# Perceiver layer on one core: the shared gated unit taken out of the per-tile periods and run tile by tile between the last tile and the experts

## The chip, the cores and the metric

The kernel runs on one core of one Trainium2 chip. The metric is the device time of the program in microseconds (us); the lower, the better. Three runs of the kernel before gave 1420.79, 1424.43 and 1424.91 us, median 1424.43 us. A further execution was profiled: every row below is from it.

## The reference, cut to what matters

The input `x` is 64 sequences of 32 rows of 256 numbers, 2048 rows in all. Each goes through cross attention to a context, a small self attention with ternary weights, and a feed-forward layer with 8 experts and one shared gated unit. Only the last matters for the change:

```python
def _moe(x, Wg, W1, W3, W2, sw1, sw3, sw2):
    ...
    probs = jax.nn.softmax(xt @ Wg, axis=-1)
    eidx = jnp.argmax(probs, axis=-1)
    ...
    pos = (jnp.cumsum(oh, axis=0) * oh).sum(-1) - 1
    keep = pos < C
    ...
    xd = jnp.zeros((E * C, d), x.dtype).at[flat].set(xt, mode='drop')
    h = jax.nn.silu(jnp.einsum('ecd,edh->ech', xd, W1)) * jnp.einsum('ecd,edh->ech', xd, W3)
    oe = jnp.einsum('ech,ehd->ecd', h, W2).reshape(E * C, d)
    ...
    shared = jax.nn.silu(xt @ sw1) * (xt @ sw3) @ sw2
    return (out + shared).reshape(b, sl, d)
```

`xt` is the normalised row. The shared unit is the line `shared = ...`, with 352 hidden columns, padded to 384. The layer's residual is added to it.

## The kernel before, in words

The 2048 rows are 16 tiles of 128 rows. Work is cut into **periods**. A prologue prepares weights and the first half of tile 0. Then 15 equal periods follow (a hardware loop on each engine), in which the first half of the next tile (keys K0 to K7, queries Q and QP, scores s0 to s3, attended values o0 to o2) is interleaved with the second half of this tile: its last entry (pt3, o3), f (output projection and residual x1), xt1, qkv, qk, sc, pv (self attention), pr (projection and residual `x2`), ln2, xt2 (the normalised rows `xn2` turned into `xn2T`), lg (router), up and dn (the shared unit), pos (the place of each row in its expert's list) and scat (an indirect DMA that puts `xn2` into the experts' rows in DRAM). The last period has the second half of tile 15 alone. Then 8 experts run one after the other: turn the rows, two products up, the gate, one product down, gather what stands in `out`, add, and put back.

Everything is hand written: each engine is in order, and its order of steps within a period is a list (`ORDER`); the steps wait on semaphores. `filled[s]` counts fills of a PSUM bank by TensorE (PE), `drained[s]` its drains. Banks are "0" to "3" (tensor AB), "4" and "5" (C), "D" (Db) and "E" (Eb).

The names that the prediction uses, by engine, with lines of the profile:

- PE: rk2, s2, o0, xt2, rk3, lg, **up** (two products into banks 4 and 5: 24 records of 128x128, `C<-xn2T,sw`), s3 (`AB<-ctxT,qpT`), pt1 (transposes `C<-consts_sb,prob` L735, and a product into Db), **dn** (`Eb<-sw,hT`, 6 records of 128x256), pos, o1 (`Eb<-pT,cn_hi`), pt2, o2, and at the next period's start K0 (`AB<-wk_hi,c_hi`).
- ACT: rk3, oh0, **up** (a sigmoid made of Exp, Ln and Exp, L1025 to L1029), e2 (four Exp of scores), ph1 (high halves of probabilities), lg, tl1 (L938, `pTl<-Db`, which drains bank D of pt1), e3, oh1, ph2.
- DVE: do0, lg (ends with `onehot`, L1650), **up** (two products, L1655 and L1658), s3 (starts with the memset of `junk` at L1307, then four products, then `nbias`), i2 (L1533, `sinv`), **dn** (L1680), dp1 (low halves, drains banks 4 and 5 of pt1), pos (ends with `slot_s`, L1675), do1, dp2, i3.
- POOL: c3, n2 (waits for i2; starts at L1124, ends with `plast` L1179; pt2 waits for it), scat (L1210), h0 of the next period (ends with `c_lo`, L1130; K0 waits for it), n3.
- SP issues the loads and, at the end of the loop's body, `store_base`: the finished rows `base` go to `out`.

In the prologue an all-zero tile, which `base` lends, clears the experts' rows in DRAM.

## Time and profile before

| what | value |
|---|---|
| median of three runs | 1424.43 us (1420.79 to 1424.91) |
| the profiled execution's own time | 1421.66 us |
| its span in the trace | 1419.8 us |
| mean granted TensorE clock | 0.962 |
| busy: PE, DVE, ACT, POOL | 89%, 65%, 62%, 40% of the span |
| matmul instructions | 10526 |
| DMA | 55.18 MB, 39 GB/s over the span |

### The profile page before, as it was taken

How to read it: one execution, taken by the hardware profiler on the slowest of the kernel's cores; microseconds unless marked ns; L12 is line 12 of the kernel's file. 1: busy time of each engine (PE TensorE's matmuls, PEld its weight loads, DVE VectorE, ACT ScalarE, POOL GpSimd, SP SyncE). 2: the span in 40 equal slices, each digit the busy share in tenths (PEclk: the TensorE clock that was granted, in tenths of full speed). 3: DMA queues.
4: the chain of work that ended last, by engine and by line, in shares of the span. 5: the costliest groups of instructions: out<-in, count | busy, mean ns of one | idle time of the engine just before them, and what ended most of it. 6: DMA issues, size and time to landing. Idle time of an engine off the chain costs nothing.

```text
span 1419.8 us, 34906 instructions
## 1 busy us (share of the span) xinstructions
PE 1270.2 (89%) x10526; PEld 853.6 (60%) x10526; DVE 916.5 (65%) x3313; ACT 884.8 (62%) x3728; POOL 574.4 (40%) x1371
## 2 busy tenths in 40 slices
PE   4877999999999999999999999999999999984596
PEld 1644666666665656666666666665656666653485
DVE  6754776767676767676776767676767676763132
ACT  4455676758576766767676758576666767661132
POOL 3044262534435352526262534435352526244143
PEclk9888999999999999999999999999999999996699
DMA  9100010101010000001010101000000001210351
GB/s 370 57 17 15 13 36 11 34 11 34 8 27 18 23 23 16 22 11 34 11 34 11 34 11 34 8 27 19 23 22 16 22 11 34 93 51 1 74 189 47
DMA packets 36130, 55.18 MB, mean 39 GB/s; under 512 B 6748, under 2 KB 29433, under 8 KB 35040
## 3 DMA queue, kind: packets, MB, share of 16 engines
q1 hardware_dynamic: 31632, 46.53, 10.5%
q0 software_dynamic: 3376, 7.98, 1.6%
q14 instruction: 52, 0.43, 0.1%
q8 instruction: 14, 0.23, 0.1%
q10 hardware_dynamic: 1056, 0.02, 0.0%
HBM read 46.54 MB, written 8.42 MB: 39 GB/s over the span
## 4 chain that ended last, share of the span: by engine, by line
PE 52%; DVE 17%; issue 9%; ACT 8%; POOL 4%; DMA 1%; POOLq 0%; DVEq 0%; ACTq 0%
PE AB L595 27%; PE Db L595 9%; PE Eb L595 7%; DVE kst L1351 3%; PE C L595 3%; DVE rq L1408 2%; PE C L720 2%; PE C L735 2%; POOL prob L1169 2%; ACT AB L946 2%; ACT prob L1014 2%; DVE pT L1538 2%; DVE px L1620 1%; ACT wt_q L938 1%; ACT rkb L1008 1%
## 5 line engine op out<-in xcount | busy, mean ns | idle before, releaser
L946 ACT ACTIVATE AB<-AB 128x128 f32<-128x128 f32 (+1 forms) x1160 | 303.3, 261 | 105.0 <-PE AB L595 101.7
L1124 POOL TENSOR_TENSOR pjunk<-pjunk 128x1 f32<-128x1 f32 x289 | 57.5, 199 | 681.4 <-DVE sinv L1533 386.4
L1351 DVE BATCH_NORM_STATS2 kst<-AB 128x6 f32<-128x256 f32 x512 | 181.7, 416 | 107.1 <-PE AB L595 102.0
L595 PE MATMUL AB<-wk_hi,c_hi 128*128 128x512 f16 x512 | 199.4, 389 | 19.1 <-POOL c_lo L1130 7.3
L946 ACT ACTIVATION_READ_ACCUMULATOR AB<-AB 128x1 f32 (+1 forms) x1160 | 215.6, 186 | 0.0
L595 PE MATMUL AB<-wk_lo,c_hi 128*128 128x512 f16 x512 | 197.8, 386 | 0.0
L595 PE MATMUL AB<-wk_hi,c_lo 128*128 128x512 f16 x512 | 197.7, 386 | 0.0
L1014 ACT ACTIVATE prob<-prob,nbias,rq 128x257 f32<-128x257 f32 x256 | 150.6, 591 | 8.4 <-DVE nbias L1528 8.4
L1169 POOL TENSOR_SCALAR prob<-prob,sinv 128x257 f32<-128x257 f32 x256 | 129.7, 507 | 20.2
L595 PE MATMUL AB<-ctxT,qpT 128*128 128x257 f32 x512 | 123.2, 383 | 11.5 <-ACT pxT L1046 11.5
L595 PEld LDWEIGHTS AB<-wk_hi,c_hi 128*128 128x128 f16 x512 | 50.9, 99 | 101.2 <-issue 29.3
L595 PEld LDWEIGHTS AB<-ctxT,qpT 128*128 128x128 f32 x512 | 92.3, 190 | 26.0 <-ACT pxT L1046 15.5
L1008 ACT COPY rkb<-C 128x512 f32<-128x512 f32 x128 | 69.3, 596 | 55.7 <-PE C L720 54.8
L595 PE MATMUL Eb<-pT,cn_hi 128*128 128x512 f16 x256 | 88.8, 386 | 8.8 <-DVE o_halves L1543 5.3
L1522 DVE CUSTOM_DVE_ANT_0 prob<-AB,rkb 128x257 f32<-128x257 f32 x256 | 94.1, 422 | 0.0
L1538 DVE TENSOR_TENSOR pT<-C,pT 128x512 f16<-128x512 f32 x128 | 82.2, 683 | 11.7 <-ACT pT L985 10.4
L595 PEld LDWEIGHTS AB<-wk_hi,c_lo 128*128 128x128 f16 x512 | 51.0, 100 | 63.1 <-issue 4.7
L595 PE MATMUL Db<-wvo_hi,o_halves 128*128 128x256 f16 x512 | 86.5, 273 | 0.7 <-ACT o_halves L978 0.7
L595 PE MATMUL AB<-x_hi,wqk_hi 128*128 128x128 f16 x512 | 86.9, 219 | 0.0
L595 PE MATMUL AB<-x_lo,wqk_hi 128*128 128x128 f16 x512 | 86.8, 219 | 0.0
L595 PE MATMUL AB<-x_hi,wqk_lo 128*128 128x128 f16 x512 | 86.8, 219 | 0.0
L735 PE MATMUL C<-consts_sb,prob 128*128 128x128 f32 x512 | 69.0, 278 | 17.8 <-POOL plast L1179 17.8
(282 smaller groups left out, 2873.9 us busy)
## 6 DMA issues: line engine op xcount, KB each, us to landing
ctxT<-in_ctxT SPq DMA_DIRECT2D x64, 128.5 KB, 2.1
ctxn<-in_ctxn SPq DMA_DIRECT2D x64, 128.0 KB, 2.1
expert_rows<-base POOLq DMA_DIRECT2D x1, 2048.0 KB, 15.6
xin<-in_x SPq DMA_DIRECT2D x16, 128.0 KB, 2.2
prob<-in_wqT SPq DMA_DIRECT2D x1, 2048.0 KB, 20.3
xres<-in_x SPq DMA_DIRECT2D x16, 128.0 KB, 2.1
out<-base SPq DMA_DIRECT2D x16, 128.0 KB, 1.7
wq_hi<-in_w SPq DMA_DIRECT2D x2, 768.0 KB, 4.5
```

Source lines behind the costliest of these rows:

```text
L595: return pe.matmul(out, lhsT, rhs, start=start, stop=stop)
L720: ins = pe.transpose(C[:, n, KT * P * (g % 2) + P * tt:KT * P * (g % 2) + P * (tt + 1)], rkx[:, b % 2, tt, P * g:P * (g + 1)], ident)
L735: ins = pe.transpose(C[:, tt, P * g:P * (g + 1)], prob[:, b, g, P * tt:P * (tt + 1)], ident)
L946: ins = nc.scalar.activation(k, k, ACT.Square, accum_out=sums[0:m, h:h + 1])
L1008: nc.scalar.copy(rkb[:, b % 2, 2 * n:2 * n + 2, 0:KT * P], C[:, n].rearrange("p (g n) -> p g n", g=2)).then_inc(drained[s].sem, 1)
L1014: ins = nc.scalar.activation(prob[:, b, g], prob[:, b, g], ACT.Exp, bias=nbias[:, b, g:g + 1], scale=rq[:, G * b + g:G * b + g + 1], accum ...
L1124: own.mark(pool.tensor_tensor(pjunk[:, 0:1], pjunk[:, 1:2], pjunk[:, 1:2], ALU.mult))
L1169: ins = pool.tensor_scalar(prob[:, b, g], prob[:, b, g], sinv[:, b, g:g + 1], P_SCALE, ALU.mult, ALU.mult)
L1351: ins = V.bn_stats(stats[:, 0, 2 * half + n], AB[0:m, 2 + half, 2 * D * n:2 * D * (n + 1)])
L1408: ins = V.tensor_scalar(rq[SQ * m:SQ * (m + 1), G * b:G * (b + 1)], src, 1.0 / WQK_SCALE, None, ALU.mult)
L1522: V.tensor_tensor_reduce(prob[:, b, g], AB[:, g, 0:SKV], rkb[:, b % 2, g], 1.0, BELOW, ALU.mult, ALU.max, smax[:, b, g:g + 1]).then_inc(dr ...
L1538: V.tensor_tensor(pT[:, b % 2, 1, tt], C[:, tt], pT[:, b % 2, 0, tt], ALU.subtract).then_inc(drained[s].sem, 1)
```

## The change

The shared unit leaves the periods. In a period only its inputs are kept: when tile n's `x2` and `xn2T` are ready, SP stores `x2` to `out` and `xn2T` to spare DRAM (`store_halfway`), where `base` was stored before. The two products up (`shared_up`, U0 to U15), the sigmoid (`shared_sigmoid`), the gate (`shared_hidden`), the product down (`shared_down`, D0 to D15) and the sum (`shared_sum`) of all 16 tiles run in the last period, in an order of its own, `LAST_ORDER`: U0 to U7 and D0 to D5 stand between the steps of tile 15, and U8 to U15 and D6 to D15 behind its last step, ahead of the experts. The operands come back from DRAM into the unused ends of four weight tensors (`turned`, `back`), four tiles ahead; the sum is written in place and stored to `out`. U uses banks 0 to 3 in pairs (U4: banks 4 and 5). The experts' rows are loaded behind D9's store. POOL's gathers wait for all 16 stores.

```diff
     "PE": """K0 pt3 K1 X K2 o3 K3 f Q xt1 K4 qkv QP rk0 s0 qk sc rk1 K5 K6 K7 pt0 pv s1 st pr rk2 s2 o0 xt2 rk3
-              lg up s3 pt1 dn pos o1 pt2 o2""".split(),
+              lg s3 pt1 pos o1 pt2 o2""".split(),
     "ACT": """K0 tl3 K1 X ph3 K2 oh3 K3 gKN0 Q xt1 gRQ K4 qkv gqkv QP rk0 qk e0 rk1 K5 sc K6 K7 ph0 gKN1 pv tl0
-              rk2 e1 xt2 rk3 oh0 up e2 ph1 lg tl1 e3 oh1 ph2 tl2 oh2""".split(),
+              rk2 e1 xt2 rk3 oh0 e2 ph1 lg tl1 e3 oh1 ph2 tl2 oh2""".split(),
     "DVE": """K0 X K1 XL dp3 K2 K3 KN0 do3 kn0 f Q RQ K4 rq qkv qr s0 sc K5 i0 sm K6 K7 KN1 dp0 kn1 ys yv s1 pr
-              ln2 i1 s2 do0 lg up s3 i2 dn dp1 pos do1 dp2 i3 do2""".split(),
+              ln2 i1 s2 do0 lg s3 i2 dp1 pos do1 dp2 i3 do2""".split(),
     "POOL": """h0 n3 h1 X h2 c0 c1 r0 cl ln1 r1 h3 n0 r2 y r3 ln2 c2 n1 c3 n2 scat""".split(),
+}
+
+
+BANK_PAIRS = ["01", "23", "01", "23", "45"] + ["01", "23"] * 6
+LAST_ORDER = {
+    "PE": """U0 pt3 U1 o3 f D0 U2 xt1 D1 qkv U3 D2 qk sc U4 D3 pv U5 st pr D4 U6 xt2 lg D5 U7 pos D6 U8 D7 U9 D8 U10 D9
+             U11 D10 U12 D11 U13 D12 U14 D13 U15 D14 D15""".split(),
+    "ACT": """tl3 ph3 U0 oh3 U1 xt1 U2 qkv gqkv U3 qk sc U4 pv U5 xt2 U6 lg U7 U8 U9 U10 U11 U12 U13 U14 U15""".split(),
+    "DVE": """dp3 U0 do3 f U1 D0 qkv U2 D1 qr U3 D2 sc sm U4 D3 ys yv pr ln2 U5 D4 lg U6 D5 pos U7 D6 U8 D7 U9 D8
+              U10 D9 U11 D10 U12 D11 U13 D12 U14 D13 U15 D14 D15""".split(),
+    "POOL": """n3 ln1 y ln2 scat""".split(),
...
+            def store_halfway(p):
+                sp.wait_ge(drained["E"].sem, drained["E"].at(p, "pr"))
+                sp.dma_start(d["out"][bass.ds(p.tile * P, P), :], x2[:]).then_inc(x2_out.sem, 16)
+                sp.wait_ge(drained["D"].sem, drained["D"].at(p, "xt2"))
+                sp.dma_start(turned_rows[bass.ds(p.tile * P, P), :], xn2T[:].rearrange("p k n -> p (k n)")).then_inc(xn2T_out.sem, 16)
...
+            def load_rows():
+                sp.wait_ge(scattered.sem, scattered.at(LAST, "scat"))
+                for e in range(E):
+                    sp.dma_start(xrows[e], xd_rows[e * CAP:(e + 1) * CAP, :].rearrange("(p a) c -> p a c", p=P))\
+                        .then_inc(rows_in[e], 16)
+
+            def load_turned(n):
+                sp.dma_start(turned[n % 4].rearrange("p k n -> p (k n)"), turned_rows[n * P:(n + 1) * P, :])\
+                    .then_inc(turned_in[n % 4], 16)
+
+            def load_back(n):
+                sp.dma_start(back[n % 4], d["out"][n * P:(n + 1) * P, :]).then_inc(back_in[n % 4], 16)
+
             sp.wait_ge(filled["3"].sem, filled["3"].at(p, "QP"))
+            for n in range(4):
+                sp.wait_ge(xn2T_out.sem, 16 * (n + 2))
+                load_turned(n)
+                sp.wait_ge(x2_out.sem, 16 * (n + 2))
+                load_back(n)
             for e in range(4):
                 load_up(e)
             sp.wait_ge(filled["3"].sem, filled["3"].at(p, "K7"))
@@ -570,11 +618,21 @@
             sp.wait_ge(filled["5"].sem, filled["5"].at(p, "rk3"))
             for e in range(2, 4):
                 load_down(e)
-            store_base(p)
-            store_base(LAST)
-            sp.wait_ge(scattered.sem, scattered.at(LAST, "scat"))
-            for e in range(E):
-                sp.dma_start(xrows[e], xd_rows[e * CAP:(e + 1) * CAP, :].rearrange("(p a) c -> p a c", p=P)).then_inc(rows_in[e], 16)
+            store_halfway(p)
+            sp.wait_ge(xn2T_out.sem, xn2T_out.at(p, "o"))
+            sp.wait_ge(x2_out.sem, x2_out.at(p, "o"))
+            for n in range(TILES):
+                s = BANK_PAIRS[n][1]
+                sp.wait_ge(filled[s].sem, filled[s].at(LAST, f"U{n}"))
+                if n + 4 < TILES - 1:
+                    load_turned(n + 4)
+                sp.wait_ge(drained["E"].sem, drained["E"].at(LAST, f"D{n}"))
+                sp.dma_start(d["out"][n * P:(n + 1) * P, :], back_of(n)).then_inc(sum_out[n % 4] if n < TILES - 1 else last_out, 16)
+                if n + 4 < TILES - 1:
+                    sp.wait_ge(sum_out[n % 4], 16 * (n // 4 + 1))
+                    load_back(n + 4)
+                if n == 9:
+                    load_rows()
...
+            def shared_up(p, n):
+                if n < TILES - 1:
+                    pe.wait_ge(turned_in[n % 4], 16 * (n // 4 + 1))
+                else:
+                    pe.wait_ge(drained["D"].sem, drained["D"].at(p, "xt2"))
+                for w, s in enumerate(BANK_PAIRS[n]):
+                    pe.wait_ge(drained[s].sem, drained[s].turn(p, f"U{n}"))
+                    up(lambda f: bank[s][:, P * f:P * (f + 1)], sw13, w, turned_of(n)).then_inc(filled[s].sem, 1)
...
+            def shared_down(p, n):
+                s = BANK_PAIRS[n][1]
+                pe.wait_ge(drained[s].sem, drained[s].at(p, f"U{n}"))
+                start(p, f"D{n}")
                 for f in range(FC):
-                    ins = mm(Eb[:, 0:DIM], hT[:, f], sw2[:, f], start=f == 0, stop=f == FC - 1)
+                    ins = mm(Eb[:, 0:DIM], uhT[n % 2][:, f], sw2[:, f], start=f == 0, stop=f == FC - 1)
...
+            def shared_sigmoid(p, n):
+                s = BANK_PAIRS[n][0]
+                act.wait_ge(filled[s].sem, filled[s].at(p, f"U{n}"))
+                if n >= 2:
+                    s2 = BANK_PAIRS[n - 2][0]
+                    act.wait_ge(drained[s2].sem, drained[s2].at(p, f"U{n - 2}"))
+                sigmoid(p, n, flat2(usig[n % 2]), bank[s][:, 0:FC * P]).then_inc(sig_ready.sem, 1)
...
+            def step_xt2(p):
+                act.wait_ge(xn2T_out.sem, xn2T_out.before(p))
+                drain(p, "xt2", "D", flat2(xn2T), Db[:, 0:DIM])
...
-            pool.wait_ge(base_out.sem, base_out.at(LAST, "o"))
+            for k in range(4):
+                pool.wait_ge(sum_out[k], 16 * len(range(k, TILES - 1, 4)))
+            pool.wait_ge(last_out, 16)
...
+                dve.wait_ge(x2_out.sem, x2_out.before(p))
...
+            def shared_hidden(p, n):
+                first, second = BANK_PAIRS[n]
+                hidden, n_cols = all_of(uhT[n % 2]), FC * P
+                dve.wait_ge(sig_ready.sem, sig_ready.at(p, f"U{n}"))
+                if n >= 2:
+                    dve.wait_ge(filled["E"].sem, filled["E"].at(p, f"D{n - 2}"))
+                V.tensor_tensor(hidden, bank[first][:, 0:n_cols], all_of(usig[n % 2]), ALU.mult).then_inc(drained[first].sem, 1)
+                dve.wait_ge(drained[first].sem, drained[first].at(p, f"U{n}"))
+                dve.wait_ge(filled[second].sem, filled[second].at(p, f"U{n}"))
+                V.tensor_tensor(hidden, hidden, bank[second][:, 0:n_cols], ALU.mult).then_inc(drained[second].sem, 1)
+
+            def shared_sum(p, n):
+                dve.wait_ge(filled["E"].sem, filled["E"].at(p, f"D{n}"))
+                if n < TILES - 1:
+                    dve.wait_ge(back_in[n % 4], 16 * (n // 4 + 1))
+                V.tensor_tensor(back_of(n), back_of(n), Eb[:, 0:DIM], ALU.add).then_inc(drained["E"].sem, 1)
```

Three places, as the order of the built programs shows them.

TensorE (PE) near the end of the loop's body, before: lg (`Db<-wg`), up, s3, pt1, dn, pos.

```order
L595 MATMUL Db<-wg,xn2T 128x8 x2
L854 REGISTER_ALU
L595 MATMUL C<-xn2T,sw 128x128 x12
L726 REGISTER_ALU
L595 MATMUL AB<-ctxT,qpT 128x257 x4
L733 REGISTER_ALU
L735 MATMUL C<-consts_sb,prob 128x128 x8
L595 MATMUL Db<-ident,plast 12x128 x4
L592 REGISTER_ALU
L595 MATMUL Eb<-sw,hT 128x256 x3
L595 MATMUL Db<-onehot,consts_sb 128x8
```

The same place in the changed program:

```order
L653 MATMUL Db<-wg,xn2T 128x8 x2
L784 REGISTER_ALU
L653 MATMUL AB<-ctxT,qpT 128x257 x4
L791 REGISTER_ALU
L793 MATMUL C<-consts_sb,prob 128x128 x8
L795 REGISTER_ALU
L653 MATMUL Db<-ident,plast 12x128 x4
L650 REGISTER_ALU
L653 MATMUL Db<-onehot,consts_sb 128x8
```

Both products of the shared unit are gone; s3 stands right behind lg, and pos right behind pt1.

VectorE (DVE) at the same place, before: the end of lg (`onehot`), up, and the start of s3.

```order
L1649 CAST eidx<-idx 128x1
L136 REGISTER_ALU
L1650 TENSOR_SCALAR onehot<-consts_sb,eidx 128x8
L1655 TENSOR_TENSOR hT<-C,sig 128x384
L1656 REGISTER_ALU
L1657 REGISTER_ALU
L1658 TENSOR_TENSOR hT<-hT,C 128x384
L1516 REGISTER_ALU
L1519 REGISTER_ALU
L1307 MEMSET junk 128x1
```

The same place in the changed program:

```order
L1725 CAST eidx<-idx 128x1
L136 REGISTER_ALU
L1726 TENSOR_SCALAR onehot<-consts_sb,eidx 128x8
L1590 REGISTER_ALU
L1591 REGISTER_ALU
L1594 REGISTER_ALU
L1382 MEMSET junk 128x1
```

s3 follows `onehot` directly. All else that stands around it on DVE is as it was.

TensorE in the last period, before, from xt1 on (`wt_q` is sc, `pxT,vals` is pv, `wproj` is pr):

```order
L604 MATMUL Eb<-consts_sb,xn 128x128 x2
L595 MATMUL Db<-wqkv,xn1T 128x384 x2
L788 MATMUL C<-consts_sb,heads 128x128 x8
L595 MATMUL AB<-wt_q 32x32 x64
L595 MATMUL AB<-pxT,vals 32x128 x16
L595 MATMUL Db<-ones,px 128x1
L595 MATMUL Eb<-wproj,pxT 128x256 x4
```

And in the changed program, from D0 on (a product of x12 into AB or C is a U, one of x3 into Eb is a D):

```order
L653 MATMUL Eb<-sw,hT 128x256 x3
L653 MATMUL AB<-wqk_hi,sw 128x128 x12
L662 MATMUL Eb<-consts_sb,xn 128x128 x2
L653 MATMUL Eb<-sw,prob 128x256 x3
L653 MATMUL Db<-wqkv,xn1T 128x384 x2
L653 MATMUL AB<-wqk_lo,sw 128x128 x12
L653 MATMUL Eb<-sw,hT 128x256 x3
L846 MATMUL C<-consts_sb,heads 128x128 x8
L653 MATMUL AB<-wt_q 32x32 x64
L653 MATMUL C<-wq_hi,sw 128x128 x12
L653 MATMUL Eb<-sw,prob 128x256 x3
L653 MATMUL AB<-pxT,vals 32x128 x16
```

A product of another tile now stands between any two steps of tile 15 but qk and sc.

## Rows read from the trace of the kernel before

**Rows 1.** The page, busy us (share of span) and instructions by engine.

```profile
PE 1270.2 (89%) x10526; PEld 853.6 (60%) x10526; DVE 916.5 (65%) x3313; ACT 884.8 (62%) x3728; POOL 574.4 (40%) x1371
```

**Rows 2.** Waits of TensorE, 268 to 1268 us: us in total, times, longest.

```profile
PE AB L595 <- POOL c_lo L1130: 6.7, 13, 0.6
```

**Rows 3.** Timeline of PE, one period's end: start, us, what [idle before].

```profile
1174.09 1.04 PE L720 MATMUL C<-consts_sb,rkx 128*128 128x128 f32 x8
...
1179.71 2.94 PE L595 MATMUL C<-xn2T,sw 128*128 128x128 f32 x24
1182.49 1.90 PE L595 MATMUL AB<-ctxT,qpT 128*128 128x257 f32 x8
...
1185.52 1.56 PE L595 MATMUL Eb<-sw,hT 128*128 128x256 f32 x6
...
1187.78 0.38 PE L595 MATMUL Eb<-pT,cn_hi 128*128 128x512 f16 x1
...
1189.63 1.09 PE L735 MATMUL C<-consts_sb,prob 128*128 128x128 f32 x8 [0.18 <-POOL plast L1179]
...
1193.28 0.39 PE L595 MATMUL AB<-wk_hi,c_hi 128*128 128x512 f16 x1 [0.39 <-POOL c_lo L1130]
```

**Rows 4.** Timeline of PE, rk2 of the following period.

```profile
1249.80 1.04 PE L720 MATMUL C<-consts_sb,rkx 128*128 128x128 f32 x8
```

**Rows 5.** Timeline of DVE at the same place.

```profile
1182.41 0.47 DVE L1650 TENSOR_SCALAR onehot<-consts_sb,eidx 128x8 f32<-128x8 f32 x1
...
1184.40 0.06 DVE L1307 MEMSET junk<- 128x1 f32 x1 [0.18 <-DVE hT L1658]
...
1186.14 0.17 DVE L1533 RECIPROCAL sinv<-ssum 128x4 f32<-128x4 f32 x1
```

**Rows 6.** Timeline of ACT at the same place: the sigmoid's last step, and tl1.

```profile
1182.43 0.52 ACT L1029 ACTIVATE sig<-sig 128x384 f32<-128x384 f32 x1
...
1186.35 0.56 ACT L938 CAST pTl<-Db 12x512 f16<-12x512 f32 x1
```

**Rows 7.** Timeline of POOL at the same place: n2's start, scat, h0's end.

```profile
1186.38 0.19 POOL L1124 TENSOR_TENSOR pjunk<-pjunk 128x1 f32<-128x1 f32 x1 [3.54 <-DVE sinv L1533]
...
1190.70 1.11 POOL L1210 DMA_INDIRECT expert_rows<-xn,slot_s  x1 [0.55 <-issue]
...
1192.47 0.68 POOL L1130 TENSOR_TENSOR c_lo<-ctxT,c_hi 128x257 f16<-128x257 f32 x1
```

**Rows 8.** Windows of PE: stretch and its us, PE busy, granted clock, DMA.

```profile
1268.00:1338.00 70.00, 31.80 (x294) 0.66 0.09 13
1157.00:1161.00 4.00, 4.00 (x15) 0.57 0.00 0
```

**Rows 9.** Timeline of PE, the last tile and the first expert.

```profile
1285.49 0.44 PE L604 MATMUL Eb<-consts_sb,xn 128*128 128x128 f32 x2 [2.48 <-DVE xn L1340]
...
1294.46 1.97 PE L788 MATMUL C<-consts_sb,heads 128*128 128x128 f32 x8 [5.81 <-DVE heads L1593]
1297.15 1.48 PE L595 MATMUL AB<-wt_q 16*32 16x32 f32 x105 [0.72 <-ACT wt_q L938]
...
1301.01 1.08 PE L595 MATMUL AB<-wt_q 16*32 16x32 f32 x18 [0.43 <-issue]
1307.78 1.05 PE L595 MATMUL AB<-pxT,vals 32*32 32x128 f32 x32 [5.68 <-DVE pxT L1615]
...
1318.26 0.69 PE L604 MATMUL Db<-consts_sb,xn 128*128 128x128 f32 x2 [2.53 <-DVE xn L1340]
...
1337.97 1.11 PE L899 MATMUL Eb<-consts_sb,rkb 128*128 128x128 f32 x4 [9.93 <-DMA rkb<-expert_rows]
1339.80 8.05 PE L595 MATMUL AB<-prob,wq_hi 128*128 128x256 f32 x24 [0.72 <-issue]
...
1349.01 5.42 PE L595 MATMUL AB<-prob,wq_lo 128*128 128x256 f32 x24 [0.72 <-ACT prob L938]
```

**Rows 10.** The page, DMA issues: KB each, median us to landing.

```profile
xin<-in_x SPq DMA_DIRECT2D x16, 128.0 KB, 2.2
```

More of the change, by code:

```diff
@@ L318, in build @@
         hT = sb("hT", [P, FC, P])
-        base = sb("base", [P, DIM])
         stats = sb("stats", [P, 6])
@@ L375, in build @@
         xres_in = Events(sem("xres_in"), 16, **fills)
-        base_out = Events(sem("base_out"), 16, pro=["none"], full=["o"], last=["o"])
+        x2_out = Events(sem("x2_out"), 16, pro=["none"], full=["o"])
+        xn2T_out = Events(sem("xn2T_out"), 16, pro=["none"], full=["o"])
+        back_in = [sem(f"back_in{k}") for k in range(4)]
+        turned_in = [sem(f"turned_in{k}") for k in range(4)]
+        sum_out = [sem(f"sum_out{k}") for k in range(4)]
+        last_out = sem("last_out")
         ctxT_in = [Events(sem(f"ctxT_in{b}"), 16, **fills) for b in range(NB)]
@@ L460, in build, with turned_of, back_of @@
         rest = [x[:, 2 * n:2 * n + 2, :].rearrange("p a n -> p (a n)") for x in (pxT, px) for n in range(8)]
+        bank = {s: AB[:, n] for n, s in enumerate(BANKS)} | {"4": C[:, 0], "5": C[:, 1]}
+        def turned_of(n):
+            return turned[n % 4] if n < TILES - 1 else xn2T
+        def back_of(n):
+            return back[n % 4] if n < TILES - 1 else x2[:]
         def wo_of(h):
@@ L1073, in _ @@
                 "pv": step_pv,
-                "xt2": lambda p: drain(p, "xt2", "D", flat2(xn2T), Db[:, 0:DIM]),
-                "lg": step_lg, "up": step_up,
-            }
+                "xt2": step_xt2,
+                "lg": step_lg,
+            }
+            for n in range(TILES):
+                steps[f"U{n}"] = lambda p, n=n: shared_sigmoid(p, n)
             steps |= {f"K{j}": (lambda p, j=j: square_keys(p, f"K{j}", P, kn2[:, H * j:H * (j + 1)])) for j in range(8)}
```

70 lines of the change are left out of this document (27 added, 43 removed).

## The prediction, made before the run

> **What bounds the kernel now.** I read the page first: TensorE is busy 89% of the span, the others 40 to 65% [rows 1]. That is a mean over three stages, so next I read one period on a timeline. From one rk2 to the next it is 1249.80 - 1174.09 = 75.7 us [rows 3, 4]. PE waits in it only in short pieces. The one that matters here is the wait of K0 for `c_lo` from POOL: 6.7 us in 13 periods, 0.5 each [rows 2]. It is short, but it says that POOL's chain ends later than PE's own at the seam of two periods: PE and a chain over DVE and POOL are nearly even there. So what leaves PE counts only as far as that chain gets shorter too. The third view is the last tile: 31.8 us busy of 70, at a mean clock of 0.66 [rows 8]; a chain of short steps with waits of 2.5 to 5.8 us between them, and 9.9 us for the experts' rows [rows 9]. There PE has room.
>
> **The periods.** At full clock up takes 1182.49 - 1179.71 = 2.78 us of PE, and dn 1.56 [rows 3]: 4.34 us per tile. Were PE alone the bound, 15 periods would give back 65.1 us. I follow the chain instead, in the times of [rows 3, 5 to 7].
> - PE: lg ends at 1179.7, s3 follows to 1181.5, pt1 to 1183.0.
> - DVE: `onehot` ends at 1182.9, as before, since do0 and lg depend on nothing that moved. s3 started at 1184.40; now at 1183.1, with the usual 0.2 us of issue. So s3 and i2 come 1.3 us earlier: `sinv` at 1184.8 for 1186.14.
> - POOL: n2 waits for i2 and starts at 1185.1 for 1186.38. It took until 1189.6, so now 1188.3. Scat waited a further 0.4 us for the slots; pos now has its input early, so scat moves by 1.7, and h0 ends at 1191.4 for 1193.15.
> - ACT: without the sigmoid (three steps of 0.5) e2 starts 2 us earlier. But tl1, which empties bank D for pos, still stands behind e2, ph1 and lg: `pTl` at about 1184.3 for 1186.35. So pos waits until 1184.9, and o1 follows to 1187.0. Its low half needs dp1, ready at 1186.2, hence no later.
> - PE again: pt2 waits for n2 until 1188.35 (before 1189.63), o2 ends at 1191.3, K0 starts with h0 at 1191.45 (before 1193.28).
>
> The seam moves by 1.8 us, not 4.3; the other 2.5 us reappear on PE as two gaps, of about 1.9 us ahead of pos and 1.3 us ahead of pt2. What comes behind K0 keeps its order and lengths. I take 1.75 per period, and 1.4 for the last one, which has no K0: 14 x 1.75 + 1.4 = **25.9 us off**. The bounds of this term: 1.3 per period (the DVE step alone), 19.5; and 4.34, 65.1. I stand near the lower one, as the row of POOL's wait [rows 2] is the nearest thing measured.
>
> The Trainium skill (Perfetto Trace Analysis, Identifying the Most-Contended Engine) says to optimise the engine with the highest occupancy first; for TensorE it distrusts that share as a distance to the limit. By the first half of this rule all 65.1 us would come off; the trace agrees on which engine is busiest, 89%, but its wait on `c_lo` speaks against the whole gain. It is a rival below.
>
> The new stores cost nothing that I can find. A 128 KB transfer lands in about 2.2 us [rows 10]; SP now issues two per period in place of one. Both sources are ready before SP comes to them (it waits for s3 first), so ctxn's last load behind them goes out earlier than behind `base`. DVE's pr and ACT's xt2 wait for the stores of the period before, landed 60 us earlier. If that cover went, a store would delay pr by its 2.2 us.
>
> **The last stretch.** I keep the old clock times, with the end of o2 at 1268.4, and lay LAST_ORDER over them. U0 fills the wait for n3; U1 ends at 1275.3; o3 and f run as before, f to 1283.0.
> - D0 and U2 stand ahead of xt1: 1283.0 + 1.56 + 2.78 = 1287.3, for 1285.49 (1.8 late). D1 stands ahead of qkv.
> - DVE does U2's gate (the 1.5 us between `onehot` and s3 in [rows 5]) and D1's sum ahead of qr: qk at 1297.1 for 1294.46 (2.6 late). sc starts at 1299.2 for 1297.15.
> - sc took 1302.09 - 1297.15 = 4.9 us, of which 1.8 are issue gaps and the rest ran at half clock; at full clock 3.3. It ends at 1302.5.
> - U4 and D3 (4.3 us) fit under the softmax; pv at 1308.2 for 1307.78.
> - U5, st, pr (half its time at full clock), D4, U6: xt2 at 1318.6 for 1318.26.
> - lg, D5, U7, pos: pos ends at 1324.7.
> - Ten D and eight U are left: 10 x 1.56 + 8 x 2.78 = 37.8 us, PE alone. ACT (three steps of 0.52, [rows 6]) and DVE (the gate's 1.5 us, and a sum that is smaller than either product) need less than the 4.3 us of a tile, and D of a tile stands behind U of the next, so their chains hide. D15 ends at 1362.7, with 0.2 of wait for its gate.
> - The experts' rows, asked for behind D9 (near 1340), land under U11 to U14, so the 9.9 us of waiting disappear. Bank E's drain, the turn and its copy take 2.0 us, and the first product up is at full clock, 5.2 us for 8.05. The turn and copy for the next take 1.3: the second expert's product starts at 1371.3, for 1349.01 before. From there all is as it was.
>
> That is **22.3 us on**. Not in it yet: around qk and sc PE does little for some 7 us, and there the clock will fall, as it did before; I add **2.5 us** (U4 and D3 partly at half clock, 4.3 us of work). Bounds of the whole term: no idle at all on PE (16 x 4.34 of shared unit, about 15.5 for tile 15 at full clock, 7.9 up to the second expert) gives 92.8 us for the stretch of 80.6, or 12.2 on; tile 15 at half clock throughout gives about 18 more than my 22.3, or 40.
>
> Loads: `turned` n + 4 is issued behind the store of tile n - 1, more than three tiles of 4.3 us ahead of its U, against 2.2 to land. The narrowest is tile 14: its load stands behind the eight loads of rows, issued near 1347, wanted near 1352.
>
> **Sum.** 1419.8 - 25.9 + 22.3 + 2.5 = 1418.7 us of span, and 1.9 around it: 1420.6. The profiled execution took 1421.66, and the median of the runs, 1424.43, is 2.8 above it; on that scale the sum would be 1423.4. I say **1421.5**: no change. A measurement of this kernel tells about 0.3% (4.3 us) from nothing.
>
> **The rivals.**
> - *The whole of PE's time comes off the periods.* For it: 89% busy, waits of a few tenths. Against it: pt2 and K0 already wait on POOL [rows 3]. It gives 1420.6 - 39.2 = 1381. Chance 0.06.
> - *The last stretch packs better* (no fall of the clock, gaps filled): down to the bound above, 1410.5; from 3.3 us of gain on it shows as faster. For it: PE has work at hand nearly everywhere. Chance 0.27.
> - *Slower: the new gaps make the clock fall in each period.* For it: the clock already fell in some periods without any long wait; at 1157 it was 0.57 over 4 us, with PE busy throughout [rows 8], right behind sc. Such a fall costs 1.7 us where PE is the bound. The two new gaps lie within 5 us of each other, and pt2, o2 behind them are on the path. At 1.5 us each, four more periods with a fall make it slower, all fifteen cost 22: up to 1443. Against it: they are shorter than the waits of 2.5 us and more behind which it fell in the last tile [rows 9], with two us of matmuls between them. Chance 0.15.
> - *Slower: the last stretch stays at 1.2 GHz* to about pos, as before, U and D then at double length: 1439. Against it: PE is now busy in most of the stretch. Chance 0.10.
> - The forecast, within 0.3%: 0.42.
>
> **How the numbers follow.** Faster 0.33 (the first two), same 0.42, slower 0.25. The range leaves out the first rival and most of the extreme ends of the two slower ones: 1404 to 1438. For the forecast alone, 1416 to 1427.
>
> **What the profile would show.** Right: a period of about 74 us; new waits of PE, for ACT's `pTl` ahead of pos and for `plast` ahead of pt2; K0 still waiting for `c_lo`; no wait for the experts' rows; 103 to 105 us from the last period's start to the second expert's product. Wrong: a period near 71.4 us (the chain had slack that I missed); granted clock below 1 around pt2 in most periods; waits of U or D on `turned` or `back`, which I put at none; issue gaps within U and D.

## The result, and the profile after

The changed kernel takes 1434.86 us (1430.49 to 1437.59, 6 runs), the kernel before in the same session 1422.61 (1420.35 to 1424.91, 6 runs): 1.0074 times, 95% interval 1.0057 to 1.0091, so 0.6 to 0.9% slower. The forecast was no change, 1421.5. The profiled execution took 1436.62 us, its span 1434.8 for 1419.8.

The page after, for [rows 1] (busy us, share of the span, instructions):

```profile
PE 1274.6 (89%) x10526; PEld 853.6 (59%) x10526; DVE 916.0 (64%) x3313; ACT 885.8 (62%) x3728; POOL 574.3 (40%) x1371
```

Shares tell nothing here: the two pages look alike. I cut both spans at DVE's step lg (its `onehot`), which every tile has, and at the second expert's first product.

| us of the profiled execution | before | after | forecast of the difference |
|---|---|---|---|
| to the first lg | 193.1 | 192.4 | 0 |
| 14 periods, lg to lg | 1065.0 | 1052.0 | -24.5 |
| last full tile's lg to the second expert's product | 90.8 | 119.6 | +23.4 |
| from there to the end | 70.8 | 70.7 | 0 |

(14 x 1.75 = 24.5; the forecast's -1.4 for the seam without K0 and its +24.8 for the last stretch make up the +23.4.) So the miss has two parts: the periods gave 11.5 us less than forecast, the last stretch cost 5.4 more. That these add up to 16.9 while the span is 16.1 above the forecast's 1418.7 is, but for rounding, the prologue's 0.7.

**The periods.** TensorE's waits after, 268 to 1250 us, for [rows 2] (us in total, times, longest):

```profile
PE Db L653 <- ACT pTl L1001: 21.6, 14, 1.9
PE C L793 <- POOL plast L1252: 20.8, 26, 1.5
PE AB L653 <- ACT wt_q L1001: 14.7, 13, 1.2
PE AB L653 <- ACT pxT L1113: 9.9, 13, 0.8
```

The two forecast gaps stand at the head of the list: for `pTl` ahead of pos (21.6 us in 14 waits, 1.5 each; forecast 1.9) and for `plast` ahead of pt2 (forecast 1.3). One thing differs from the forecast: PE no longer waits for `c_lo` ahead of K0. POOL's chain and PE's own now end together there, and the wait that bounds the period's end is the one for `plast`. The timeline of PE at one period's end, for [rows 3]:

```profile
1170.77 0.39 PE L653 MATMUL Db<-onehot,consts_sb 128*128 128x8 f32 x2 [1.45 <-ACT pTl L1001]
...
1174.58 1.09 PE L793 MATMUL C<-consts_sb,prob 128*128 128x128 f32 x8 [1.49 <-POOL plast L1252]
```

Periods in which the clock held are 74.0 us (median of 3) for 75.7 before (median of 10): 1.67 less, for 1.75 forecast. But only 3 of 14 held. In 11 the granted clock fell from 2.4 to 1.2 GHz, in the kernel before in 4, and within these periods it fell at one place, right behind sc. PE around such a fall, first the timeline, then windows (us from and to; us; busy time and instructions of PE, PEld, DVE, ACT, POOL; granted clock; DMA share; GB/s):

```profile
1066.37 1.28 PE L653 MATMUL AB<-wt_q 16*32 16x32 f32 x128 [1.12 <-ACT wt_q L1001]
1067.58 1.91 PE L778 MATMUL C<-consts_sb,rkx 128*128 128x128 f32 x8
1069.28 0.63 PE L653 MATMUL AB<-wk_hi,c_hi 128*128 128x512 f16 x1
```

```profile
1065.00:1067.50 2.50, 1.38 (x131) 1.17 (x129) 0.60 (x5) 2.50 (x7) 0.00 (x0) 1.00 0.15 45
1067.50:1071.00 3.50, 3.50 (x30) 2.29 (x18) 2.27 (x6) 2.17 (x8) 0.00 (x0) 0.53 0.00 0
1071.00:1074.00 3.00, 3.00 (x15) 1.42 (x14) 1.67 (x6) 3.00 (x20) 0.09 (x1) 0.98 0.00 0
```

PE waits 1.12 us for `wt_q`, then does 128 tiny products of 16x32 in 1.28 us, and then its clock is at 1.2 GHz for some 3.4 us with PE busy throughout. Both kernels have this place; nothing there was changed. 14 periods at 74.0 would be 1036; they took 1052, so the falls cost 16 us. In the kernel before 14 x 75.7 = 1060 stand against 1065: 5 us.

**The last stretch.** It begins with a fall that the count of 14 periods leaves out: behind the two new gaps of the last full tile the clock is at 1.2 GHz for 6.8 us, and from lg to the end of o2 it takes 11.2 us, where 10.3 less the forecast 1.4 had been laid out. That is 2.3 of the 5.4 us.

```profile
1250.07 1.97 PE L793 MATMUL C<-consts_sb,prob 128*128 128x128 f32 x8 [0.71 <-POOL plast L1252]
```

```profile
1248.60:1255.40 6.80, 6.09 (x22) 3.10 (x20) 2.49 (x7) 2.88 (x7) 4.01 (x11) 0.50 0.05 16
```

From there PE's walk went as laid out as far as qk, and then stopped:

```profile
1284.28 1.09 PE L846 MATMUL C<-consts_sb,heads 128*128 128x128 f32 x8 [1.63 <-issue]
1295.01 1.53 PE L653 MATMUL AB<-wt_q 16*32 16x32 f32 x128 [9.64 <-ACT wt_q L1001]
```

PE waits for ACT, but qk had been done since 1285.4. ACT, DVE and POOL at the same time:

```profile
1281.24 0.52 ACT L1092 ACTIVATE prob<-prob 128x384 f32<-128x384 f32 x1
1293.84 1.07 ACT L1001 COPY wt_q<-C 128x512 f32<-128x512 f32 x2 [12.08 <-remote]
```

```profile
1293.78 0.55 DVE L1737 TENSOR_TENSOR prob<-prob,AB 128x384 f32<-128x384 f32 x1 [9.08 <-remote]
```

```profile
1272.27 1.11 POOL L1287 DMA_INDIRECT expert_out<-tag,slots  x1 [0.16 <-issue]
...
1290.36 0.97 POOL L1287 DMA_INDIRECT expert_out<-tag,slots  x1 [0.30 <-issue]
```

ACT and DVE resume within 0.1 us of each other. "remote" means that the profile names no engine of the program as the releaser. All the while, until 1291.3, POOL writes the tags of tiles 0 to 14 (a tag tells the experts which token stands in a row, and its gate), one small indirect DMA every 1.28 us. SP's store of tile 1's sum was followed by the load that waits for it only 8.2 us later; in f1_no_tags below, without the fifteen writes, the same two stand 1.7 us apart.

```profile
1281.00 0.34 SPq L630 DMA_DIRECT2D out<-wq_lo  x1
1289.21 0.33 SPq L605 DMA_DIRECT2D wq_lo<-out  x1
```

The kernel before writes the same tags at the same point of its last tile; what they cost there is taken up below, with the experiments on the tags.

The rest of the stretch was close. Counted from the end of o2, pos ended 7.2 us later than laid out (63.5 us for 56.3). From pos to the end of D15 it took 36.5 us for 38.0: the unit took 2.68 + 1.30 us per tile on PE instead of 4.34, which over the last eight U and ten D is 34.4 us for 37.8, and some 2 us of waits stood between them. The experts' rows were waited for no more, and tile 14's `turned` came late by 0.8 us, the load named as the narrowest. 7.2 less 1.5, less the 2.5 us that the forecast had added for the clock, are the other 3.1 of the 5.4 us.

```profile
1345.13 2.94 PE L653 MATMUL AB<-wqk_hi,sw 128*128 128x128 f32 x24 [0.82 <-DMA wqk_hi<-expert_out]
...
1364.07 5.42 PE L653 MATMUL AB<-prob,wq_lo 128*128 128x256 f32 x24 [0.72 <-ACT prob L1001]
```

### The profile page after: what moved, and what is told of

Read it like the earlier page. It is cut to its first block, busy times and chain, and to the rows that moved or that the text cites. A ratio compares the mean times of both kernels' runs of the same rounds, so it can differ in the third digit from the quotient of the medians.

```text
span 1434.8 us, 35151 instructions
## 1 busy us (share of the span) xinstructions
PE 1274.6 (89%) x10526; PEld 853.6 (59%) x10526; DVE 916.0 (64%) x3313; ACT 885.8 (62%) x3728; POOL 574.3 (40%) x1371
## 4 chain that ended last, share of the span: by engine, by line
PE 42%; DVE 15%; POOL 13%; issue 13%; ACT 6%; DMA 1%; another core or an unknown queue 1%; POOLq 1%; SPq 0%; DVEq 0%; ACTq 0%
PE AB L653 26%; PE Db L653 8%; POOL prob L1242 6%; DVE kst L1426 3%; PE Eb L653 3%; DVE rq L1483 2%; POOL pjunk L1197 2%; PE C L778 1%; POOL cn_lo L1262 1%; PE C L793 1%; ACT AB L1009 1%; ACT wt_q L1001 1%; DVE px L1695 1%; DVE prob L1597 1%
## 5 line engine op out<-in xcount | busy, mean ns | idle before, releaser
L1426 DVE BATCH_NORM_STATS2 kst<-AB 128x6 f32<-128x256 f32 x512 | 181.8, 417 | 110.4 <-PE AB L653 105.7
L653 PE MATMUL AB<-ctxT,qpT 128*128 128x257 f32 x512 | 124.4, 386 | 11.5 <-ACT pxT L1113 11.5
L1071 ACT COPY rkb<-C 128x512 f32<-128x512 f32 x128 | 70.3, 597 | 63.5 <-PE C L778 62.5
L793 PEld LDWEIGHTS C<-consts_sb,prob 128*128 128x128 f32 x512 | 57.5, 143 | 59.0 <-POOL plast L1252 38.2
```

The costliest lines, as they stand in the source:

```text
L653: return pe.matmul(out, lhsT, rhs, start=start, stop=stop)
L793: ins = pe.transpose(C[:, tt, P * g:P * (g + 1)], prob[:, b, g, P * tt:P * (tt + 1)], ident)
L1071: nc.scalar.copy(rkb[:, b % 2, 2 * n:2 * n + 2, 0:KT * P], C[:, n].rearrange("p (g n) -> p g n", g=2)).then_inc(drained[s].sem, 1)
L1426: ins = V.bn_stats(stats[:, 0, 2 * half + n], AB[0:m, 2 + half, 2 * D * n:2 * D * (n + 1)])
```

## The experiments

Theories when they began. A: in the periods, falls of the clock behind sc ate what the moved unit gave. B: in the last tile, the tag writes hold up ACT, DVE and the transfers. Rivals: the two new gaps are what costs (the prediction's own rival); the stop comes of code fetched for the long unrolled stretch, or of the unit's loads and stores. The table has all runs. The e and f runs, the g runs, the h runs and i1 were made on four different chips, and each ratio is to the kernel before on the same chip; the last four columns are from one profiled execution each. "Held" is the median of the periods without a fall, "falls" those in 14 periods, in brackets those behind sc, "tail" is from lg of the last full tile to the second expert's product.

| run | time, us | ratio to before, 95% | period mean | held | falls | tail |
|---|---|---|---|---|---|---|
| before | 1422.6 to 1425.3 | 1 | 76.07 | 75.69 | 4 (4) | 90.8 |
| after | 1434.86 | 1.0057 to 1.0091 | 75.14 | 74.01 | 11 (11) | 119.6 |
| e0_again | 1435.53 | 1.0046 to 1.0080 | 75.34 | 74.21 | 12 (11) | 118.0 |
| e1_filler | 1420.30 | 0.9956 to 0.9983 | 74.34 | 74.01 | 8 (0) | 118.1 |
| e1_filler_before | 1418.36 | 0.9939 to 0.9967 | 75.70 | 75.69 | 0 | 96.3 |
| e2_tags_late | 1444.27 | 1.0120 to 1.0155 | 75.34 | 73.85 | 13 (10) | 123.3 |
| f1_no_tags | 1421.31 | 0.9966 to 0.9995 | 75.11 | 74.04 | 11 (11) | 111.0 |
| f2_tags_each | 1430.39 | 1.0019 to 1.0045 | 75.36 | 75.18 | 2 (1) | 110.4 |
| e3_s3_first | 1417.97 | 0.9946 to 0.9985 | 73.83 | 72.86 | 10 (6) | 116.9 |
| f3_best | 1415.23 | 0.9915 to 0.9946 | 74.30 | 74.10 | 9 (0) | 109.6 |
| g_before_s3 | 1535.61 | 1.0754 to 1.0808 | 83.62 | none | 21 (7) | 98.6 |
| g_best_before | 1510.89 | 1.0578 to 1.0628 | 82.21 | 82.51 | 13 (0) | 90.5 |
| g_best | 1402.23 | 0.9805 to 0.9858 | 73.54 | 72.78 | 8 (0) | 108.0 |
| g_best2 | 1392.25 | 0.9752 to 0.9804 | 72.95 | 72.91 | 0 | 106.8 |
| h1_before_tags_filler | 1411.42 | 0.9891 to 0.9926 | 75.52 | 75.50 | 0 | 88.1 |
| h2_before_late_up | 1470.28 | 1.0307 to 1.0337 | 79.26 | 78.64 | 6 (3) | 98.1 |
| h3_before_late_up_all | 1454.22 | 1.0204 to 1.0237 | 78.72 | 78.38 | 2 (0) | 87.9 |
| i1_tags_filler | 1415.48 | 0.9908 to 0.9959 | 74.15 | 74.04 | 6 (0) | 110.8 |

### The clock behind sc: e0_again, e1_filler, e1_filler_before

e0_again is the changed kernel unaltered. The other two add idle products to step qk, in the changed kernel and in the one before:

```diff
+                if p.kind == "full":
+                    for _ in range(4):
+                        mm(Eb[:], wvo_hi[:, 0, 0:P], wvo_hi[:, 0:2].rearrange("p h n -> p (h n)"))
```

> The changed kernel, unaltered, for a second profile. Two things in its first profile are in question: 11 falls of the granted clock to 0.5 in the 15 periods, all within 24.4 to 25.5 us ahead of lg (behind sc), and one stretch near 1285 to 1294 us in which ACT and DVE both stood still for 9 us. Theory: both belong to the kernel; again 8 to 13 falls at that place, and again a stop of some us while POOL writes the tags. Rival: the stop was an accident of one execution, and is absent here. Time 1430 to 1437 us in either case, with the stop 5 to 9 us more than without.

> The changed kernel with four idle 512-column products on TensorE between qk and sc of each full period, into bank E, which nobody reads; they take 0.9 us of the 1.1 us in which TensorE waits for ACT there. Theory (clock falls behind sc cost the missing time): falls in the periods drop from 11 to 0 to 2, the mean period from 75.1 to about 74.1 us, the time by 10 to 15 us to about 1421. Rival 1 (the doubled stores or other traffic hold the periods): falls or not, periods stay at 75.1, no change. Rival 2 (the falls come from the new gaps ahead of pos and pt2): no change in their number.

> The kernel before with the same four idle products in each full period. It had 4 falls behind sc in 15 periods, periods of 77.0 us with one and 75.7 without. Theory: no fall, all periods 75.7 us, 4 x 1.3 = 5 us less than before, about 1417.5. Rival (the falls are not made by that wait): no change, or slower by what the products cost, up to 14 x 0.9 = 12 us, if the wait is not really free.

The falls behind sc and the stop repeat in e0_again; it also has one fall behind the new gap ahead of pos, of 6.8 us, in a period that took 77.7 us. The idle products (1.03 us) take up most of the wait for `wt_q`, and no fall behind sc is left; PE in e1_filler:

```profile
1058.50 1.03 PE L653 MATMUL Eb<-wvo_hi 128*128 128x512 f16 x4
1059.78 1.28 PE L653 MATMUL AB<-wt_q 16*32 16x32 f32 x128 [0.26 <-issue]
1060.99 1.09 PE L778 MATMUL C<-consts_sb,rkx 128*128 128x128 f32 x8
```

15 us come back in the changed kernel and 6.5 in the one before, which had 11 falls and 4. Held periods stay as long as they were (74.01 and 75.69), so it is the falls that went, and theory A holds. The rival is not nothing: 8 falls remain, where none to two had been expected. They begin 2.4 to 4.1 us behind `onehot`, right behind the new gap ahead of pos, and cost 0.3 us per period in the mean.

### The tags: e2_tags_late, f1_no_tags, f2_tags_each

```diff
 # e2_tags_late, in last_norm and last_rows
-                    for n in range(TILES - 1):
-                        put_tags(n)
...
-                    put_tags(TILES - 1)
+                    for n in range(TILES):
+                        put_tags(n)
 # f1_no_tags: the loop over TILES - 1 left out, and ACT's wait for tagged 16 * 2
 # f2_tags_each, in last_rows of every period
                 scatter(p)
+                put_tag()        # slot_s and a tile's own tag_s
```

> The changed kernel with the 15 small indirect writes of tags moved from POOL's ln1 of the last tile to behind its scatter. Theory (these writes hold up the transfers and with them ACT and DVE in the last tile): the 9 us stop ahead of sc is gone, pos 7 us earlier after the last period's start, time 5 to 9 us less than the changed kernel, about 1427. Rival (the stop has another cause or is an accident): same time as the changed kernel within 3 us. A third possibility: the stop moves with the writes into the products behind pos, and nothing is won.

> The changed kernel without the fifteen writes of the tags in the last tile (the experts then have no token for those tiles' rows, so their part of the output is left out; the last tile's tag stays). Theory: these writes, issued on POOL every 1.28 us while the shared unit's loads, stores and sums run, are what holds ACT 12.1 us and DVE 9.1 us ahead of sc. Without them sc starts some 7 to 9 us earlier and from the end of o2 to the second expert's product there are some 100 us instead of 108.5; the periods are untouched; in all 1426 to 1428. Rival: what holds the engines there is code that is fetched for the unrolled last stretch, or the 1.3 MB per 10 us of loads and stores; then the stop stays where it was, with 8 us or more, and the time is 1434 to 1436.

> The changed kernel with each tile's tags written in its own period, right behind the rows' scatter, instead of fifteen writes in the last tile. POOL issues one more write of 1.0 to 1.3 us per period at a place where it is mostly ahead; whole output. If a tag write costs ACT and DVE some 0.6 us (9.1 us over 15) wherever it stands and the periods have no cover, nothing is gained: 1434 to 1436. If the periods have cover for it, the gain of the kernel without the writes comes in full: 1426 to 1428. If POOL's write behind the scatter delays h0 and so K0 of the next period by its 1.3 us, the periods lose up to 14 x 1.3 = 18 us: up to 1445.

With the tags behind the scatter the wait ahead of sc is gone, but ACT stops for 5.4 and 14.8 us behind pos, while they are being written or just after: 9 us slower, its expectation's third case and worse. Without them (the experts then lack tiles 0 to 14) both stops are gone; ACT in f1_no_tags, at the same place:

```profile
1276.46 0.52 ACT L1092 ACTIVATE prob<-prob 128x384 f32<-128x384 f32 x1
1280.37 1.07 ACT L1001 COPY wt_q<-C 128x512 f32<-128x512 f32 x2 [3.38 <-PE C L846]
```

From lg to lg the last tile takes 63.3 us instead of 71.4. The unrolled code and the unit's loads and stores are the same in both, so neither of them makes the stop of 8.1 us by itself: it needs the tags. Of the run's other gains in the profiled span 4.2 us lie ahead of the first lg (188.2 us for 192.4), where nothing was changed; the starts of the runs spread from 188.2 to 197.0. Another 1.0 lies in the experts, where the tokens of tiles 0 to 14 are missing.

The stop is not new with the move. In the last tile of the kernel before, it strikes TensorE in the middle of sc, whose 128 products then come in pieces with "issue" ahead of them. First e1_filler_before, then h1_before_tags_filler, the same kernel with the fifteen writes taken out of the last tile (see below):

```profile
1294.17 1.04 PE L595 MATMUL AB<-wt_q 16*32 16x32 f32 x41 [0.72 <-issue]
...
1299.87 0.28 PE L595 MATMUL AB<-wt_q 16*32 16x32 f32 x3 [1.78 <-issue]
...
1303.43 1.26 PE L595 MATMUL AB<-wt_q 16*32 16x32 f32 x71 [1.12 <-issue]
```

```profile
1290.40 1.54 PE L596 MATMUL AB<-wt_q 16*32 16x32 f32 x128 [0.72 <-ACT wt_q L942]
```

```profile
1290.40:1291.90 1.50, 1.50 (x128) 1.40 (x128) 0.00 (x0) 0.00 (x0) 0.00 (x0) 0.50 0.05 11
```

These 128 products took 4.9 us in the kernel before and 10.3 to 10.5 in its variants e1_filler_before, g_before_s3 and h2, all with the fifteen writes there; they took 1.5 in h1, h3 and g_best_before, without them. The tails are 90.8 to 98.6 us with the writes and 87.9 to 90.5 without. So the tags cost both kernels several us, and little else needs to move beside them: from 1283 to 1304 e1_filler_before moved 2 GB/s in all. How a tag write holds engines that issue no DMA is not shown. That it holds up the fetch of their code is a rival that no run here excludes.

f2_tags_each has the stop gone too, with all the work done, but pays 1.2 us per period (75.18 for 74.01): POOL issues the tag between scat and h0, and K0 waits for h0. POOL there, and PE's wait, 268 to 1220 us, which the changed kernel did not have:

```profile
1103.39 1.10 POOL L1284 DMA_INDIRECT expert_rows<-xn,slot_s  x1 [0.55 <-issue]
1104.79 0.99 POOL L1288 DMA_INDIRECT expert_out<-tag_s,slot_s  x1 [0.30 <-issue]
```

```profile
PE AB L654 <- POOL c_lo L1204: 14.4, 12, 1.2
```

Of its expectation neither of the first two cases came, but the third in size (14 x 1.2 = 16 us), offset by something not expected: at 75.2 us the periods had 2 falls and not 11, which gives back some 13 (1.44 us each), and the tail is 9 us shorter: 1434.8 + 16 - 13 - 9 = 1429, the span measured is 1428.9.

### The seam: e3_s3_first, f3_best

```diff
-              lg s3 pt1 pos o1 pt2 o2""".split(),
+              s3 lg pt1 pos o1 pt2 o2""".split(),
-              ln2 i1 s2 do0 lg s3 i2 dp1 pos do1 dp2 i3 do2""".split(),
+              ln2 i1 s2 do0 s3 i2 lg dp1 pos do1 dp2 i3 do2""".split(),
```

> The changed kernel with PE's scores s3 ahead of the gate's product lg, and DVE's s3 and i2 ahead of its lg. The second of the two new gaps (PE's 1.5 us wait for POOL's plast ahead of pt2, 14 per run) should close, since the last softmax group of the tile starts some 1.9 us earlier; K0 comes about 1.0 us earlier. Theory: 1.0 us less per undisturbed period (73.1 instead of 74.1), 15 us in all, so 1419 to 1421 if the clock falls as often as in the changed kernel (11 times). Rival: only the gap moves (to lg's wait for the positions, which now start later), and periods stay at 74.1: 1434 to 1436. What the other period length does to the falls behind sc is open: if they go, another 11 x 1.2 us less, if they come in every period, 4 us more.

> The changed kernel with three edits together: four idle products of 512 columns behind qk (14 us less when alone), s3 ahead of lg (expected 0 to 15 less) and the tags written in each period (expected 0 to 8 less). If all three add up: 1435 - 15 - 12 - 7 = 1401. If the reorder and the tags give nothing: 1420, as with the idle products alone.

1.15 us less per held period: the prediction's chain from s3 over i2 and n2 bounds the seam indeed, and an earlier s3 shortens it further. PE's waits in e3_s3_first, 268 to 1230 us; `pTl` has left the list and `plast` is down from 20.8:

```profile
PE Db L653 <- DVE onehot L1726: 11.2, 14, 0.9
...
PE Db L653 <- DVE lgs L1718: 9.6, 13, 0.7
PE C L793 <- POOL plast L1252: 5.8, 22, 0.4
```

f3_best has the idle products behind qk, this order and the tags of f2_tags_each, and still held periods of 74.1: the tag behind the scatter takes the 1.2 us back (g_best below has it elsewhere and 72.8), because it stands on the very chain that the reorder shortened. The three edits didn't add up.

### The repairs together, on both kernels: g_best, g_best2, g_before_s3, g_best_before

g_best is f3_best with the tags of a tile written one period later, where POOL waits for DVE anyhow; g_best2 has idle products ahead of pos too. g_before_s3 is the kernel before with the new order alone, g_best_before with that order, the idle products behind qk and the tags in POOL's wait:

```diff
-    "POOL": """h0 n3 h1 X h2 c0 c1 r0 cl ...
+    "POOL": """h0 n3 h1 X h2 c0 c1 tag r0 cl ...
 # g_best2, ahead of the waits in step_pos
+                if p.kind == "full":
+                    pe.wait_ge(drained["E"].sem, drained["E"].turn(p, "o1"))
+                    for _ in range(6):
+                        mm(Eb[:], wvo_hi[:, 0, 0:P], wvo_hi[:, 0:2].rearrange("p h n -> p (h n)"))
 # g_before_s3, g_best_before: the kernel before with
-              lg up s3 pt1 dn pos o1 pt2 o2
+              s3 lg up pt1 dn pos o1 pt2 o2
-              ln2 i1 s2 do0 lg up s3 i2 dn dp1 pos ...
+              ln2 i1 s2 do0 s3 i2 lg up dn dp1 pos ...
```

> The changed kernel with s3 ahead of lg, four idle products behind qk, and the tags in POOL's wait between c1 and r0 of the next period. Undisturbed periods should be the 72.8 of the reorder alone plus nothing for the tags (they had been 74.0 with the tags behind the scatter), the stop ahead of sc gone as in the kernel without tags: 1413.6 - 14 x 1.1 = 1398 for the span, 1400 for the time. Rival: a tag write costs its 1.0 us per period wherever it stands, through the transfers and not through POOL: then 1414 to 1416 again.

> As g_best, with six more idle products of 512 columns ahead of the positions, where PE waits 0.75 and 0.77 us and where 9 of the 10 remaining falls of the clock begin. If those waits make the clock fall, the falls at a period's end go, and 9 x 0.5 to 1.2 us with them, less up to 0.5 us per period that the products take beyond the waits: 1392 to 1400. If they don't, the falls stay and the products cost 14 x 0.5 = 7 us: 1405 to 1408.

> The kernel before, unit left in its periods, with only the order at a period's end changed: PE's s3 ahead of lg, up; DVE's s3 and i2 ahead of lg, up, dn. If what the periods gained (74.1 instead of 75.7) came from s3 being 1.75 us earlier than before, the reorder alone brings it, with none of the last stretch's 22 to 28 us: periods of 73.5 to 74.5 undisturbed, 14 x 1.6 = 22 us less, 1398 to 1405. Rival: PE needs the unit's 4.34 us in the periods anyhow, so moving s3 ahead only moves the wait for POOL's c_lo into another (the positions, the hidden layer's sigmoid): periods stay at 75.0 to 75.7, 1415 to 1425.

> As g_before_s3, with four idle products of 512 columns behind qk (6.5 us less when alone) and each tile's tags written one period later, between POOL's c1 and r0, where POOL waits 8.4 us for DVE (the kernel behind the scatter paid 1.0 us per period). If the three add up: 1400 - 5 - 4 = about 1391; if the reorder gives nothing: 1412 to 1416.

The tags cost nothing there: held periods of 72.78 for 72.86 without them. POOL in g_best2, with the wait behind the tag:

```profile
1085.36 1.09 POOL L1295 DMA_INDIRECT expert_out<-tag_s,slot_s  x1 [0.17 <-issue]
1093.42 0.18 POOL L1205 TENSOR_TENSOR pjunk<-pjunk 128x1 f32<-128x1 f32 x1 [6.96 <-DVE rk L1409]
```

In g_best all 8 falls begin 0.3 to 2.1 us behind `onehot`, at or right behind two waits of 0.7 and 0.8 us ahead of pos. In g_best2 six idle products stand in the second of them:

```profile
1069.90 1.47 PE L654 MATMUL Eb<-wvo_hi 128*128 128x512 f16 x6
1071.20 0.28 PE L654 MATMUL Db<-onehot,consts_sb 128*128 128x8 f32 x2
```

No fall is left in any period, each takes 72.7 to 73.6 us, and the kernel takes 1392.25 us, 2.0 to 2.5% less than before and 3% less than the changed one. So even waits of 0.7 and 0.8 us, with a few short products between and behind them, can cost the clock.

The same order of steps in the kernel before, with the unit left in, is 7.8% slower, which neither case of its expectation allowed for; g_best_before, expected at 1391 to 1416, is 6.0% slower. PE in g_before_s3:

```profile
688.84 2.92 PE L595 MATMUL C<-xn2T,sw 128*128 128x128 f32 x24
...
696.56 1.97 PE L735 MATMUL C<-consts_sb,prob 128*128 128x128 f32 x8 [4.79 <-DVE hT L1655]
```

```profile
692.00:696.50 4.50, 0.00 (x0) 0.00 (x0) 1.87 (x11) 2.41 (x9) 1.56 (x4) 0.77 0.00 0
696.50:703.00 6.50, 6.09 (x26) 4.67 (x27) 1.88 (x5) 4.19 (x13) 1.15 (x5) 0.64 0.00 0
```

pt1 needs the unit's two banks, which are free only when the hidden layer has been read, and s3 no longer covers that time. Its periods are 7.9 us longer: 4.8 us of wait, and some 3 more, put down here to the fall of the clock that begins in this wait and not tested by itself.

### What the move itself is worth: h1, h2, h3, i1

h1_before_tags_filler and i1_tags_filler are the kernel before and the changed kernel, both in their own order of steps, with the idle products behind qk and the tags in POOL's wait. h2_before_late_up keeps the unit but puts s3 where the changed kernel has it; h3_before_late_up_all is h2 with the idle products and the tags in POOL's wait:

```diff
-              lg up s3 pt1 dn pos o1 pt2 o2""".split(),
+              lg s3 pt1 up pos o1 dn pt2 o2""".split(),
-              rk2 e1 xt2 rk3 oh0 up e2 ph1 lg tl1 e3 oh1 ...
+              rk2 e1 xt2 rk3 oh0 e2 ph1 lg tl1 e3 up oh1 ...
-              ln2 i1 s2 do0 lg up s3 i2 dn dp1 pos do1 dp2 ...
+              ln2 i1 s2 do0 lg s3 i2 dp1 up pos do1 dn dp2 ...
```

> The kernel before with its order of steps unaltered, four idle products behind qk (alone 6.5 us less), and each tile's tags written in POOL's wait between c1 and r0 of the next period. It is the fair partner of the changed kernel with the same two edits. Its last tile held ACT up 4.6 us behind qk while the fifteen tags were written; without them some 3 to 6 us less: 1412 to 1415. If tags cost nothing in this kernel's last tile, 1418.

> The kernel before with the unit kept in the periods but issued later: PE lg s3 pt1 up pos o1 dn pt2 o2, ACT's sigmoid behind e3, DVE's hidden layer behind dp1 and the base behind do1. s3 stands where the changed kernel has it, and pt1 no longer waits for the hidden layer to leave its banks (4.8 us each time with s3 ahead of lg and up). If the changed kernel's 1.6 us per period came from the place of s3 alone: 74.1 per undisturbed period, 1400 to 1405. If it came from the unit's leaving (its banks, and ACT's and DVE's 3 to 4 us of work on it in the chain's way): pt2 or pos waits for the hidden layer instead, periods of 76 or more, 1425 or more.

> As h2, with the idle products behind qk and the tags in POOL's wait. Whatever h2 gives, less 8 to 12 us.

> The changed kernel, order of steps unaltered, with four idle products behind qk and the tags in POOL's wait: the equal partner of the kernel before with these two edits, which took 1411.4. From the idle products alone (1420.3) less the stop of 8.1 in the last tile: 1412. Then the move itself is worth nothing measurable (14 x 1.5 us in the periods against 22 us of unit work behind the tile). If it comes under 1408, the move pays once the clock and the tags are out of the way; if over 1416, the tag writes cost the periods something after all.

h2 moves the wait to the other side, 78.6 us per held period; its waits of PE, 268 to 1250 us:

```profile
PE C L595 <- DVE pT L1538: 30.8, 13, 2.6
PE Eb L595 <- DVE o_halves L1543: 18.5, 13, 1.4
```

h3 is 16 us under h2, where 8 to 12 had been expected. So in neither of the two orders tried does the kernel before get s3 earlier for nothing: what the changed kernel gained per period, 1.67 us, comes, as far as these two orders show, of the unit's leaving with its banks. (h1's expectation took ACT's 4.6 us ahead of `wt_q` in the kernel before for the tags' work; h1 has the same 4.6 without them, and what went is the time inside sc.) h1 and i1 are not told apart: 0.9891 to 0.9926 and 0.9908 to 0.9959. i1's executions go from 1406.4 us at a mean granted clock of 0.984 to 1419.3 at 0.966; h1, with no fall in its profiled periods, from 1408.4 to 1411.6. So with the same two repairs the move is worth nothing that can be measured, as had been forecast for the kernels without them; in held periods it gives 14 x 1.46 = 20 us, and the tail takes 23. What it is worth beyond that is the freedom for the order of g_best2, some 1.3% under h1 (0.9778 to 0.9908). g_best2 has idle products ahead of pos that h1 lacks, but h1 had no fall left for them to prevent.

## Why the prediction was wrong

- **The term of the periods, 14 x 1.75 us**, is the one that failed, and not by its mechanism: 1.67 per held period was measured, by the chain that the prediction followed, with both gaps at their places and about 1.5 us each for 1.9 and 1.3. (Only its last sign, K0 still waiting for `c_lo`, did not show.) What failed is the silent assumption that the clock falls as often after as before, a cost put at nothing. Falls went from 4 to 11 and took 11 of the 23 us back.
- **The rival "the new gaps make the clock fall in each period"** had its row, [rows 8], and a chance of 0.15. The row was the right one, the place mostly wrong: the prediction saw that the clock had fallen behind sc and argued about the new gaps instead. In the two profiled executions of the changed kernel 22 falls lie behind sc and two at the new gaps, one in a period of e0_again and one at the last full tile's end. The gaps matter more once sc's place is filled (e1_filler, g_best).
- **The last stretch, +24.8 us** (+23.4 as the table counts): 28.8 came, 5.4 more. 2.3 of these are the fall at the last full tile's end. From there the walk was right to within a us up to qk; then the tags stopped it for 8.1 us, a cost on POOL that the walk of three engines had left out. Its trace had it in [rows 9]: of the 4.9 us of sc the prediction put 1.8 to issue gaps and the rest to the half clock, and took 3.3 for the full clock. h1 did the same 128 products at a granted clock of 0.50 in 1.54 us, so 3.4 of the 4.9 came with the tags. The sc laid out too long, the unit's 3.98 us per tile for 4.34, and the 2.5 us added for the clock hid most of the stop.
- **"The new stores cost nothing"** and **"no wait for the experts' rows"** held; the named narrowest load was late by 0.8 us.
- **All of PE's 4.34 us off the periods** did not come; nor did the last stretch at 1.2 GHz.
- 1434.9 us lies within the stated 1404 to 1438, but not by merit: the upper end was set by two rivals, and neither came as described.
